# Ternary network of a fused eight-stage kernel: when the next stage's context masks are made, and how the normalised input is split

## The reference, cut to what matters

```python
# stage 6: _L2_ffn_ref on _layernorm(x)
wq_gu = ternary_quant(w_gate_up)            # (2048, 256), three values per group of 64
gu = jnp.einsum('bsd,hd->bsh', x, wq_gu)
gate, up = jnp.split(gu, 2, axis=-1)        # 1024 each
h = jax.nn.silu(gate) * up
hn = rms_norm(h)                            # over the 1024 hidden channels
out = jnp.einsum('bsh,dh->bsd', hn, ternary_quant(w_proj))

# stage 7: _L3_xattn_ref on _layernorm(x), with q = x, k = v = ctx
scaled = jnp.einsum('bsd,bse->bde', q, k) * scale    # per batch item, 64 tokens
attn = jax.nn.softmax(scaled, axis=1)
out = jnp.einsum('bde,bse->bsd', attn, v)

x = x + out                                 # after each stage
```

## Time and profile before

| | |
|---|---|
| median of three runs | 937.26 us (936.35 to 938.79) |
| the profiled execution, its own time | 935.47 us |
| its span from first to last instruction | 933.6 us |
| busy in the span: TensorE, VectorE, ScalarE, GpSimd | 655.1, 517.3, 283.5, 248.4 us |
| power of the norm of stage 6 ends | 506.2 us after the start of the span |
| first matmul of gate and up | 520.2 us |
| last projection added to the residual | 598.5 us |

### The profile page before, as it was taken

One profiled execution on the slowest core, in us unless ns is written; L12 is line 12 of the kernel. 1 busy time (PEld: TensorE's weight loads), 2 busy tenths in 40 slices (PEclk: granted clock), 3 DMA queues, 4 the chain that ended last, 5 costly groups with the idle time before them and its releaser, 6 DMA issues.

```text
span 933.6 us, 10770 instructions
## 1 busy us (share of the span) xinstructions
PE 655.1 (70%) x3645; PEld 416.0 (45%) x3660; DVE 517.3 (55%) x1050; ACT 283.5 (30%) x510; POOL 248.4 (27%) x230
## 2 busy tenths in 40 slices
PE   1003888878863146887863899775289999999991
PEld 1002345654552113443432466543246666666661
DVE  5786687586957887877885522356612222222223
ACT  1701233234434403554572432143021121121110
POOL 2432332147800091044466000200012211211100
PEclk9555998799957556998896799997589999999997
DMA  6000002000204422343121000396400100100004
GB/s 226 0 0 0 1 2 68 1 1 1 57 1 105 124 102 74 115 130 107 48 71 34 1 1 1 116 427 284 165 29 24 34 22 22 34 22 22 29 12 147
DMA packets 33652, 62.02 MB, mean 66 GB/s; under 512 B 5720, under 2 KB 29272, under 8 KB 31256
## 3 DMA queue, kind: packets, MB, share of 16 engines
q1 hardware_dynamic: 21752, 45.78, 14.5%
q10 hardware_dynamic: 9648, 9.64, 3.3%
q0 software_dynamic: 2208, 6.03, 2.1%
HBM read 47.54 MB, written 13.70 MB: 66 GB/s over the span
## 4 chain that ended last, share of the span: by engine, by line
PE 49%; DVE 18%; issue 6%; DMA 5%; POOL 4%; ACT 3%; SPq 0%; ACTq 0%; POOLq 0%; DVEq 0%
PE bank L1648 15%; PE bank L1669 7%; PE bank L1288 5%; DVE region L1088 3%; PE bank L1307 3%; PE bank L540 3%; PE bank L949 2%; DVE XN L347 2%; DMA channel_maxima<-region 2%; PE bank L1659 2%; PE bank L514 2%; PE bank L989 2%; PE bank L526 1%; ACT region L1347 1%; PE bank L973 1%
## 5 line engine op out<-in xcount | busy, mean ns | idle before, releaser
L1648 PE MATMUL bank<-region,wide 128*128 x368 | 143.7, 544 | 0.3 <-issue 0.3
L1552 DVE TENSOR_TENSOR wide<-wide,bank 128x448 f32<-128x448 f32 x46 | 28.6, 622 | 124.9 <-ACT wide L1595 78.5
L1648 PEld LDWEIGHTS bank<-region,wide 128*128 128x128 f32 x368 | 68.8, 192 | 61.4 <-issue 61.3
L1088 DVE TENSOR_REDUCE region<-bank 128x2 f32<-128x512 f32 x128 | 81.6, 684 | 25.8 <-PE bank L949 24.4
L949 PE MATMUL bank<-region 128*128 128x256 bf16 x256 | 57.6, 318 | 40.8 <-DMA region<-norm_parts 25.7
L1012 ACT ACTIVATE region<-bank 128x1024 f32<-128x1024 f32 x64 | 65.6, 1025 | 58.7 <-PE bank L973 51.6
L1669 PE MATMUL bank<-region,XN 128*128 x322 | 73.4, 379 | 1.2 <-DVE wide L1565 1.2
L1456 POOL DMA_INDIRECT choice_results<-wide,to_row x23 | 22.8, 990 | 181.4 <-DVE wide L1565 181.4
L1669 PEld LDWEIGHTS bank<-region,XN 128*128 128x128 f32 x322 | 59.5, 190 | 9.3 <-issue 2.1
L1595 ACT ACTIVATE wide<-bank 128x448 f32<-128x448 f32 x46 | 25.0, 544 | 111.9 <-PE bank L1648 111.9
L1780 PE MATMUL bank<-ident,XN 128*128 128x128 f32 x96 | 21.5, 414 | 48.6 <-DVE XN L347 42.0
(11 more groups left out here) (295 smaller groups left out, 1241.7 us busy)
## 6 DMA issues: line engine op xcount, KB each, us to landing
region<-in_L_ffn_experts_dram SPq DMA_DIRECT2D x8, 2688.0 KB, 19.1
region<-ctx_parts SPq DMA_DIRECT2D x24, 192.0 KB
region<-norm_parts SPq DMA_DIRECT2D x8, 576.0 KB
channel_values<-wide ACTq DMA_DIRECT2D x8, 512.0 KB, 6.3
ctx_parts<-region SPq DMA_DIRECT2D x40, 64.0 KB, 2.1
wide<-in_L_ffn_w_gate_up_dram ACTq DMA_DIRECT2D x4, 512.0 KB, 4.2
wide<-channel_values SPq DMA_DIRECT2D x16, 128.0 KB, 2.6
norm_parts<-region SPq DMA_DIRECT2D x24, 64.0 KB, 2.5
```

The costliest lines, as they stand in the source:

```text
L1088: e.tensor_reduce(nmax[i % 2][:, at_:at_ + KC], ps(u).rearrange("p (c n) -> p c n", c=KC), AX.X, ALU.max, negate=True).then_inc(s_chan["ma ...
L1552: e.tensor_tensor(HB8[par][:, cols], silu8[:, cols], bank[hf][:, 512:512 + I8 // 2], ALU.mult)\
L1648: last = e.matmul(bank[hf][:, 512 * gu:512 * gu + hw], xbT[par][:, P * c:P * c + P], region[:, bass.ds(off + (2 * gu + c) * I8 + hw * hf, ...
```

## The change

Two edits. The split is made tile by tile: an instruction covers 2 blocks of 128 = 256 elements instead of 1024. The parts of tile 0 come ahead of the loop, those of tile i+1 at the start of `hidden(i)`, and `gate_up(i)` waits for i+1 splits. The masks move on GpSimd from behind the norm's power to behind the inverse root of tile 6 (`NT - 2`), and so stand ahead of that of tile 7; what they wait for is now the last split.

```diff
@@ vec_ternary
-            for hf in range(2):
-                e.wait_ge(s_turned, TURN["tern"] + 2 * hf + 2)
-                cols = slice(512 * hf, 512 * hf + 512)
+            def parts(i):
+                e.wait_ge(s_turned, TURN["tern"] + KC * (1 + i // 4))
+                cols = slice(P * i, P * i + P)
                 split3(e, ch, XT6[:, :, cols], x6rest[:, :, cols], [a[:, :, cols] for a in x6]).then_inc(s_tern["norm_split"], 1)
 
+            parts(0)
+
             def hidden(i):
+                if i + 1 < NT:
+                    parts(i + 1)
                 for hf in range(2):
                     e.wait_ge(s_tern["silu_ready"], 2 * i + hf + 1)
@@ pool_masks
-            e.wait_ge(s_rstd, 6)
+            e.wait_ge(s_tern["norm_split"], NT)
             ch.link(e.memset(C1[0:T, :], 0.0))
@@ pool_ternary
             pool_norm(e, 5)
-            pool_masks(e, ch)
             for i in range(NT):
                 e.wait_ge(s_tern["mean_square"], i + 1)
                 e.tensor_tensor(sinv[:, i:i + 1], ssq[:, i:i + 1], half_neg[:, 0:1], ALU.pow).then_inc(s_tern["rms_inverted"], 1)
+                if i == NT - 2:
+                    pool_masks(e, ch)
@@ pe_ternary, gate_up(i)
-                e.wait_ge(s_tern["norm_split"], 1 + i // 4)
+                e.wait_ge(s_tern["norm_split"], i + 1)
```

## The result

The changed kernel took 925.93 us, median of four runs (924.33 to 929.25), beside 936.81 us for the kernel before (934.36 to 938.79, four runs): ratio 0.9897 with a 95% interval of 0.9868 to 0.9926. Times 937.26, the median that the prediction starts from, the ratio gives 927.6; the median itself lies 3.3 us under the 929.2 predicted and 0.8 under the low end. Timed twice more the ratio was 0.9890 (0.9856 to 0.9923) and 0.9902 (0.9864 to 0.9940). What makes these ratios larger than what the traces show is taken up in "What is left".

The account below looks back on a forecast made before the run. It took 14 us of serial work before the first gate-up matmul, with TensorE doing only transposes, as the bound; 4.75 + 2.82 + 0.5 = 8.1 us off 937.26 gives 929.2 us, range 926.7 to 932.2.

Parts of the forecast that it names:

- Masks leave the norm: Norm of stage 6: without GpSimd's masks, first normalised tile to first transpose takes 1.44 us instead of 6.19; gain 4.75 us.
- The first split: Ahead of the gate-up loop: the split of tile 0 takes 1.86 us instead of 4.68; gain 2.82 us.
- The start of TensorE: Before the first gate-up matmul: 0.47 us of issue, putting it at 512.65 instead of 520.22, 7.57 us earlier.
- The loop: Seven splits of 1.86 us fit VectorE's 2.40 us idle before each step's first product, 0.54 left; cost 0.
- rival C: VectorE at each step's start: splits delay TensorE once one lasts over 7.8 us; kernel slower, 940.1 us; chance 3%.
- The masks at their new place: End of the stage: masks done with 3.8 us to spare before the last `add`; cost 0, other end 1 us.
- The clock: First gate-up matmuls: shorter TensorE idle time may keep the raised clock; gain 0.5 us, between 1.6 gained and 0.8 lost.

Follow-up runs that it names:

- scalar_copy: The changed kernel with ScalarE making the masks' copy beside VectorE's normalising instructions, GpSimd keeping the two clears at the end; 930.05 us, one run.
- masks_after_norm: The changed kernel with GpSimd making all three masks once the normalised tiles are written, beside the split of tile 0; 932.04 us, ratio 0.9962.
- splits_x4: The changed kernel with each split inside the loop made four times over, same results; 936.13 us, one run.
- masks_in_loop: The changed kernel with the masks behind the inverse root of tile 0 instead of tile 6, waiting for the norm's power; 929.71 us, ratio 0.9938.

## Why the prediction held, step by step

**Masks leave the norm: right, and shown.** Predicted 4.75 us; 6.19 - 1.43 = 4.76. The row before stage 8 gave the undisturbed distance to 0.01 us. `scalar_copy` and `masks_after_norm` show that it is GpSimd, and that one VectorE instruction gets through per GpSimd instruction.

**The first split: right.** Predicted 1.86 us for two blocks of 128, measured 1.86; predicted that the fourth turned group ends 0.18 us before it, measured 508.35 - 508.17 = 0.18. Gain 2.82 against 2.80.

**The start of TensorE.** I set 0.47 us of issue at both ends, and it fell out of the difference: 7.57 predicted, 13.60 - 6.04 = 7.56 measured. That was luck: 0.37 of it was a missing record and no cost of the kernel.

**The loop: right in what it costs, wrong in its limit.** Predicted 0.54 us left before the first product, measured 0.63, and no wait of TensorE. The price of rival C, a threshold at a split of 7.8 us, came from two idle times added up. It ignored that VectorE's other work of the step comes behind the products. In `splits_x4` TensorE waited at 7.48 us; counted whole, the limit is an estimated 6.1 us, and the 2.86 us of work in 9 that would have shown it stand in the earlier trace rows. The splits of 1.86 us stay well under either.

**The masks at their new place: right, and safer than I said.** 3.9 us to spare against 3.8. I left 0.2 us for the copy on the assumption that each VectorE instruction might be held; none was. The Trainium skill, "SBUF — State Buffer", section "Who interferes with whom", says that a VectorE instruction with at most one SBUF input, outside the modes in which it uses both pairs of ports, does not contend with GpSimd; the copy out of PSUM agrees (0.69 us beside GpSimd's copy), and `add`, which reads PSUM, `X` and one column of `region`, wasn't held either (0.48 us). The small mean square, which I had let that rule hold up, wasn't held (0.14 us). The half of the rule that whoever came first holds the ports can't be seen in the rows: in `masks_in_loop`, as the profile has the starts, the cast of 0.29 us starts at 528.63 and GpSimd's clear at 528.68, and it is the cast that takes 2.01 us.

**The clock: the mechanism seen once, the size not borne out.** I took 0.5 us between 1.6 gained and 0.8 lost, as if the short idle time kept the clock about every second time. It did in one of seven traces. From the first gate-up matmul to the last `add` that one takes 76.3 us, and five of the other six 78.2 to 78.6 (the seventh is `splits_x4`); the mean of the six is 78.0, against 91.76 - 13.60 = 78.2 and 91.27 - 13.60 = 77.7 in the kernel before, where the clock rose 3.9 and 2.9 us into the matmuls. So the term measured about nothing, within the 0.5 us by which the two profiles before differ. From first L347 to last `add` the change gives 91.5 - 83.6 = 7.9 us by the three profiles of the changed kernel and 91.5 - 84.0 = 7.5 by all six. That the sum of 8.1 lies so near is in part chance; its 7.57 is what the runs bear out.

**What is left.** 8.1 predicted, 7.5 to 7.9 in the stretches, 9.6 us by the first ratio (7 to 12 by its interval), and the raw median of 925.93 even lies under the predicted range. All three ratios of the change, and those of its halves (5.8 and 4.4 us), lie some 1 to 2.5 us past their traces. Most of that goes with the mean granted clock that is on record for every execution. Executions fall into groups by it, for the kernel before as well, and the quickest lies some 5 us under the slower ones (the kernel before as it was timed beside the experiments, the changed kernel in its three timings; medians and, in brackets, counts):

```
mean granted clock   before (70 executions)   changed (16)       difference
below 0.86           936.75 us (37)           928.78 us (4)      8.0
0.86 to 0.88         937.15 us (18)           929.54 us (2)      7.6
0.88 and more        932.07 us (15)           924.44 us (10)     7.6
```

Like with like the change gives 7.6 to 8.0 us, which is what the traces give. (The mean is itself moved by the change, by an estimated 0.003, as 7.6 us at 0.50 fall out of it, and some groups are small.) The rest of the ratios is that 10 of 16 executions of the changed kernel fell in the quickest group and 15 of 70 of the kernel before. Whether that is chance or whether the change has a hand in it, is not shown.

## What to carry to other kernels

Look at what GpSimd does beside a row of VectorE instructions on the path to TensorE: here its work on memory, 1.8 to 1.9 us an instruction, let one VectorE instruction from memory to memory through for each of its own, so move such work to where VectorE's waited-for instructions read PSUM or where nobody waits, or give it to ScalarE, as `scalar_copy` did with the copy (84.23 us to the last `add` against 84.37). Before a pipelined loop, prepare only what its first turn needs and do the rest inside, once one step's whole work on that engine, not just one idle time, leaves room. Compare traces from an event at which both kernels are still the same, check the count of records before believing a gap, and compare medians among executions of like mean clock.

## What I had not expected of the hardware

The start of this stage varied by 5.9 us (502.4 to 508.3) among eleven traces of kernels that do the same up to there, which is three quarters of what the change gives. From 23 to 93 us the kernel before had a granted 0.50 in its first profile where the changed one had 1.00, and in the second profiles it was the other way round. And a quicker clock in one stage, held by idle-time matmuls, shortened its stretch by 2.8 us twice and the kernel not at all.
